# ViT tower with expert routing on one core: the bias row written in 30 pieces, and tile 2 embedded before tile 0's transposes

## The reference

```python
proj = jnp.einsum('bnk,dk->bnd', patches, W) + b               # 768 -> 256
h = jnp.concatenate([cls, proj], axis=1) + pos_embedding
# block: x = _layernorm(h); xn = layer_norm(x, ln1_w, ln1_b)
q, k, v = xn @ q_w.T + q_b, xn @ k_w.T + k_b, xn @ v_w.T + v_b  # 16 heads of 16
q, k = elu(q) + 1, elu(k) + 1
# linear attention over the heads of one token, then o_w, o_b, residual
x = x + attn
x = x + (gelu(layer_norm(x, ln2_w, ln2_b) @ fc_w.T + fc_b) @ proj_w.T + proj_b)
h = h + x
# 16 experts, each takes its top 148 tokens by softmax score, plus a shared expert
h = h + ffn(_layernorm(h))
```

## Time and profile before

| | us |
|---|---|
| median of 3 timed runs | 445.96 |
| lowest, highest | 445.86, 448.19 |
| the profiled execution | 442.74 |
| its span (first to last instruction) | 440.8 |
| busy: PE, DVE, ACT, POOL | 414.1, 352.9, 290.7, 210.7 |
| mean granted TensorE clock | 0.98 |

### The profile page before, as it was taken

One profiled execution on the slowest core, in us unless ns is written; L12 is line 12 of the kernel. 1 busy time (PEld: TensorE's weight loads), 2 busy tenths in 40 slices (PEclk: granted clock), 3 DMA queues, 4 the chain that ended last, 5 costly groups with the idle time before them and its releaser, 6 DMA issues. The chain is left out here.

```text
span 440.8 us, 11326 instructions
## 1 busy us (share of the span) xinstructions
PE 414.1 (94%) x4168; PEld 368.6 (84%) x4168; DVE 352.9 (80%) x614; ACT 290.7 (66%) x746; POOL 210.7 (48%) x238
## 2 busy tenths in 40 slices
PE   7799999999999998998999999999999999999980
PEld 3477888888988887896778799999999999999980
DVE  3799999899999998327997588888887888888830
ACT  3465576987897774776540166667777777888840
POOL 1337555776457025322350424555555666666222
PEclk9899999999999998999999999999999999999995
DMA  8802592000000000004302389889898999996411
GB/s 275 312 33 71 173 336 82 14 0 13 13 13 1 13 13 0 15 26 188 118 1 96 118 295 306 300 291 320 305 301 276 333 327 329 327 328 225 118 17 15
DMA packets 21057, 69.84 MB, mean 158 GB/s; under 512 B 4666, under 2 KB 11812, under 8 KB 14620
## 3 DMA queue, kind: packets, MB, share of 16 engines
q1 hardware_dynamic: 14828, 60.92, 38.7%
q0 software_dynamic: 4608, 5.41, 6.1%
q10 hardware_dynamic: 1584, 3.03, 1.8%
HBM read 64.02 MB, written 5.33 MB: 157 GB/s over the span
## 5 line engine op out<-in xcount | busy, mean ns | idle before, releaser
L622 POOL DMA_INDIRECT xg<-token_rows,slot_g x32 | 50.1, 1566 | 72.0 <-DVE slot_g L1401 46.5
L633 POOL DMA_INDIRECT out_rows<-scratch,slot_s x32 | 53.4, 1668 | 25.2 <-ACT scratch L982 16.7
L951 ACT ACTIVATE scratch<-bank 128x296 f32<-128x296 f32 x64 | 26.5, 414 | 43.1 <-PE bank L1896 43.1
L1896 PE MATMUL bank<-scratch,wfc_s 128*128 128x148 f16 x512 | 52.5, 228 | 1.1 <-DVE scratch L1300 1.1
L1896 PE MATMUL bank<-scratch,wsh_s 128*128 128x148 f16 x512 | 52.7, 228 | 0.0
L1896 PE MATMUL bank<-scratch,wproj_s 128*128 128x148 f16 x256 | 50.6, 227 | 0.0
L1921 PE MATMUL bank<-scratch,wex_s 128*128 128x148 f32 x312 | 47.5, 296 | 0.0
L1250 DVE SCALAR_TENSOR_TENSOR wproj_s<-wex_s,wfc_s 128x512 f16<-128x512 f32 x64 | 42.1, 686 | 5.6 <-ACT wfc_s L840 4.5
L1424 DVE SCALAR_TENSOR_TENSOR scratch<-bank,scratch 128x296 f32<-128x296 f32 x64 | 29.6, 462 | 20.4 <-ACT scratch L951 20.3
L1896 PEld LDWEIGHTS bank<-scratch,wfc_s 128*128 128x128 f16 x512 | 42.0, 97 | 1.7 <-issue 1.2
L1896 PEld LDWEIGHTS bank<-scratch,wsh_s 128*128 128x128 f16 x512 | 42.1, 97 | 0.5
(11 more groups left out here) (233 smaller groups left out, 1034.3 us busy)
## 6 DMA issues: line engine op xcount, KB each, us to landing
wex_s<-in_wex SPq DMA_DIRECT2D x48, 1024.0 KB, 5.1
patch_s<-in_patches SPq DMA_DIRECT2D x6, 384.0 KB, 3.1
token_rows<-y_s SPq DMA_DIRECT2D x10, 128.0 KB, 1.7
out_rows<-h_all SPq DMA_DIRECT2D x5, 256.0 KB, 5.3
wex_s<-in_wfc ACTq DMA_DIRECT2D x2, 512.0 KB, 9.4
wproj_s<-in_wproj SPq DMA_DIRECT2D x1, 1024.0 KB, 6.9
wex_s<-in_wsh SPq DMA_DIRECT2D x1, 1024.0 KB, 6.3
wqkv_s<-in_wqkv ACTq DMA_DIRECT2D x1, 768.0 KB, 8.2
```

The source lines that it names most:

```text
L622: gp.indirect_dma_start(xg[s.par][:, k, :], None, rows, bass.IndirectOffsetOnAxis(slot_g[s.par][:, k:k + 1], 0))\
L633: gp.indirect_dma_start(out, bass.IndirectOffsetOnAxis(slot_s[s.par][:, k:k + 1], 0), eo[2 * s.par + k], None, compute_op=ALU.add).then_in ...
L1896: last = pe.matmul(dst[p % 2][:, x * C:(x + 1) * C], w16(s.par, a, piece)[:, lo:lo + P], x16[s.par][b][:, k, :], start=(n == 0), stop=(n = ...
```

## The change

Two things are moved or reshaped.

1. The bias row lies in SBUF as 10 partitions of 128 numbers, not 128 of 10. The load has 10 rows of 512 bytes, DVE's casts and subtractions work on 10 x 128, and the write to `parts` has 3 x 10 = 30 contiguous pieces of 256 bytes, not 3 x 128 = 384 of 20. SP's wait for it and the write go ahead of the load of tile 2's patches.
2. On PE `embed(2)` goes ahead of the wait for the constants and of tile 0's transposes; before it stood behind tile 0's projections.

```diff
-        braw, brest = sb("braw", [P, BIASES // P]), sb("brest", [P, BIASES // P])
-        bpart = sb("bpart", [P, len(PARTS), BIASES // P], BF16)
+        braw, brest = sb("braw", [BIASES // P, P]), sb("brest", [BIASES // P, P])
+        bpart = sb("bpart", [BIASES // P, len(PARTS), P], BF16)
...
             sp.dma_start(patch_s[1][:, 0:half, :], patches[1, :, 0:half, :]).then_inc(patch_in[1], 16)
+            sp.wait_ge(bias_made, 5)
+            sp.dma_start(parts.rearrange("n (p j) -> p n j", j=P), bpart[:]).then_inc(bias_out, 16)
             sp.dma_start(raw_patch[2], patches[2]).then_inc(raw_in[2], 16)
-            sp.wait_ge(bias_made, 5)
-            sp.dma_start(parts.rearrange("n (p j) -> p n j", p=P), bpart[:]).then_inc(bias_out, 16)
             sp.wait_ge(ones_made, 2)
...
             embed_first()
             embed(1)
+            embed(2)
             pe.wait_ge(w_in["consts"], 32)
             turn_xh(Step(0, 0))
             keep_busy(3)
...
             project_v(Step(0, 0))
-            embed(2)
             turn_xh(Step(0, 1))
             embed(3)
...
-    a["bias"] = np.concatenate(bs + [f["L0_attn_o_b"], f["L0_attn_proj_b"]]).reshape(P, -1)
+    a["bias"] = np.concatenate(bs + [f["L0_attn_o_b"], f["L0_attn_proj_b"]]).reshape(-1, P)
```

## The result

| | before | this |
|---|---|---|
| median, us | 445.49 | 448.87 |
| lowest, highest | 444.05, 448.19 | 447.75, 451.73 |
| the profiled execution, us | 442.74 | 448.77 |
| its span, us | 440.8 | 446.8 |

11 runs of each. The ratio is 1.0086, 95% interval 1.0062 to 1.0111 (it is taken over all runs and need not be that of the medians): the change makes the kernel **slower by 3.4 us** in the medians. The forecast was 1.5 us faster, with 446.9 as the end of the range.

The account below looks back on a forecast made before the run. PE was busy 94%, DVE 80%, with DVE's chain from combine carrying the shift. Bias pieces 0, embed(2) 0, clock -1.5, MLP weights 0 took 442.74 to 441.2; 3.2 carried over gave 444.5 us, range 442.8 to 446.9.

Parts of the forecast that it names:

- The bias write: SP's write of the bias row in 30 pieces lands at 9.1 us, bounds 8.0 and 10.5.
- The marks: SP's load that embed(2) needs, issued at 10.1 us, lands at 13.2 to 14.1, taken as 13.8.
- that receipt: Time from the marks' last packets to their landing, put at 0.4 to 1 us.
- Tile 2's patches: SP's load, issued at 5.9 us, lands at 10.5 to 11; DVE wants it at 11.86, cost nothing.
- The clock: With embed(2) in PE's hole before tile 0's transposes, PE stays at 2.4 GHz throughout, gain 1.5 us.
- The prize: 1.5 us on the path: tile 0's projection to negation takes 3.67 us, tile 1's at full clock 2.13.
- What carries the shift: A shift of DVE's chain, starting at combine of tile 0, reaches the end whole; gain 1.5 us.
- Rival E: All of PE's relief counts and DVE's waits of 1.1 and 0.6 us go: -3.2, 442.8 us; chance 0.15.
- B: PE's clock falls in a new hole after the v projection, 0.6 us of gain left, 445.4; chance 0.14.
- C: DMA receipts slow under load, marks there at 15.8 us: 446.3, up to 447.8; chance 0.12.
- D: Bias write still lands at 14.3, marks at about 18.2, transposes 4.2 late: +3 to +5, 449 to 451; chance 0.09.
- The decision point: Each microsecond the marks come after 13.9 us is one on the path; from 15.4 the gain is used up.

Follow-up runs that it names:

- e5: The full change with the marks' load ahead of the three bias reads, still behind the wait for the bias write; 1.0058 of the kernel before.
- e6: The full change with ACT's two wfc loads asked for only after tile 0 is copied; 1.0088 of the kernel before.
- e12: e6 again, the full change with late wfc loads; 1.0136 of the kernel before.
- e11: e6 with DVE waiting for POOL's scale of tile 1 before its first product; 1.0037 of the kernel before.
- e3: The kernel before with 11 matmuls nobody reads behind embed(1) on PE; 0.9969 of the kernel before.
- e8: e4 with DVE waiting for POOL's scale of tile 1, and 8 unread matmuls behind tile 0's v projection; 1.0012 of the kernel before.
- e9: The change without moved embed(2), first_shift ahead of halving tile 2, 8 unread matmuls behind embed(1), DVE waiting for POOL's tile 1 scale; 0.9988 of the kernel before.
- e4: The full change with the marks' load right behind tile 2's patches, ahead of the wait for the bias write; 1.0061 of the kernel before.
- e15: The change without moved embed(2), with 16 unread matmuls behind embed(1) on PE; 0.9992 of the kernel before.
- e2: The kernel before with embed(2) moved alone, bias row still in 384 pieces; 1.0107 of the kernel before.

## Why the prediction was wrong

- **The bias write.** "I take it as landed at 9.1", reads at 9.2, marks issued at 10.1: measured 9.2, 9.24, 10.10. Right. Both parts of the edit count: the trace of before moves the 384 pieces from 8.81 to 13.73 (4.9 us, where I had counted 3.3), the change its 30 from 7.44 to 8.44 (1.0, counted 0.5), and 1.4 us come from the earlier first piece.
- **The marks.** "Now issued at 10.1, with ACT's rows between theirs, the marks need 2.1 to 3 us and that receipt: 13.2 to 14.1." **This is the step that failed.** The receipt was right, 0.83 us. The 2.1 to 3 us ran from the issue to the last row, and that took 5.9: 3.5 us to the first row, 2.4 for the rows (13.62 to 16.00). The trace of before has 1.0 and 1.4 for the two (issue 15.31, rows 16.28 to 17.71). The sum allowed for slower rows and had no term for a first row that comes 2.5 us later. The earlier trace rows had both queues moving piece for piece, and I took from them that a new request joins the turns at once; those rows show only requests that were made long before. `e5` and `e6` show the term: it doesn't depend on the bias reads in front, and shrinks to 1.0 (1.4 and 1.6 in `e12` and `e11`) when ACT's `wfc` is asked for later. What makes it stays open. A row that warned was there: tile 2's patches took 6.9 us for 384 KB, tile 1's half 6.1 for 192, so the time was in the waiting and not in the bytes.
- **Tile 2's patches.** "10.5 to 11 ... Cost nothing." They landed at 11.8, DVE waited 0.97 us, and `first_shift` came at 13.30 though DVE was 1.1 us earlier than before with its first casts. A small miss that kept `xh` from coming earlier; it cost nothing against before. DVE's bias casts on 10 x 128 took 0.21 us and its subtractions 0.28, near the 0.22 of the earlier trace rows.
- **The clock.** The prize was right in size (3.67 to 2.13 us at the projection) and on the path (`e3`, -1.4 us). But it needed the hole filled. The forecast took over the end of `embed(1)`, 13.66, from before; it came at 12.10, so that even marks at 13.8 would have left 1.7 us idle where it had "no idle stretch over 0.5 us". With the marks missing the hole grew to 4.8 us and the clock fell in front of `embed(2)`: the half rate was paid on another line, 1.93 us.
- **What carries the shift.** "A shift of DVE's chain should reach the end whole": +3.17 at `combine`, +3.16 at the first sums, +2.8 at the last product, 3.4 in the medians. Right for this delay, and it is why the loss is not smaller. For gains the runs show less: in `e8` and `e9` the last product comes 1.0 and 1.8 us earlier than in the trace of before, and their medians are 0.3 over and 0.7 under that kernel's on their chip. As the stretch behind the last product differs by some 4 us between single executions, and no trace of before was taken on that chip, what became of these gains stays open. Rival E's relief did come at one place: DVE's wait at L1100 fell from 0.6 to 0.2.
- **The rivals.** B did not come in the change (clock 1.00 from 21 us on) but in `e4`, where the marks were in time: 0.7 us at the first sums. C had the marks late at 15.8, a microsecond short of 16.83, and for the wrong reason: receipts were short (the bias write's last piece at 8.44, its landing at 9.17). D came true in its outcome (transposes 4.67 late, 1.5 back, +3.2; it had 4.2 late and +3 to +5), though the bias write, which it blamed, was early. I priced D at 0.09 because I tied it to that one cause. The decision point, marks later than 15.4, was right; any cause of a late load would have done, and the rows of other loads under the same traffic, 6.1 to 9.4 us each, were not used as its bound. The range should have reached over it.

## What to carry to other kernels

Before a step is put in front of others, take its loads' time from issue to landing from a load asked for under the same traffic, not from the bytes and the queue's rate: the first row can be what takes longest. A hole on PE whose only harm is the clock is filled more safely with matmuls that depend on nothing than with real work that waits for a load, as long as the filler ends before the hole does (`e3` gained, the overlong filler of `e15` did not). When a change moves one engine by a few tenths and runs split into two groups, look for two engines that start within those tenths, and for short instructions that last exactly as long as a long one beside them.

## What the runs showed of the hardware that was not expected

- Loads asked for by SP at 9.2 to 10.1 us moved no row until 12.7 to 13.6 while ACT's earlier and larger ones ran, although SP's own queue had moved its last earlier row at 11.05. The first of them starts 3.35 to 3.5 us after its issue in six kernels; with ACT's `wfc` asked for late the marks start after 1.0 to 1.6 us. The same 117 rows of 2 KB took 3.1 us from issue to landing with little else moving (`e2`), 5.0 with `wfc` asked for late, 6.7 in the change.
- A POOL instruction on one number per partition takes 0.19 to 0.55 us alone and 2.0 to 2.5 beside a 2.29 us product of DVE with two SBUF inputs.
- The clock does not come back at once: in the change PE is busy from 16.92 without a pause, and all of `embed(2)`, 4 us, runs at 1.2 GHz (granted clock 0.50 at 18 to 20 us).
